# Layer-norm moments, roots and scaling of early row tiles made by the preceding stage at four boundaries of a 17-stage kernel, and the recurrence's projections reordered

## Chip, cores and metric

One core of a Trainium2 chip runs the whole kernel as one program. The metric is the device time of one execution in microseconds (us). Its engines are PE (TensorE, matmuls; PEld is its weight load), DVE (VectorE), ACT (ScalarE), POOL (GpSimd) and SP (SyncE, which here only issues DMAs and clears semaphores).

## What is computed

Two layers over 16 sequences of 64 rows, width 256 (1024 rows in all), with 16 heads of 16 channels. Every one of the six sub-layers starts from a layer norm (without or with gain) of the current `x`:

```python
x = x + cross_attention(ctx, layernorm(x), Wq, Wk, Wv, Wo, bo)      # stage a0
x = x + gated_recurrence(layernorm(x), ...)                          # p2, r1, r2
x = x + ffn(layernorm(x)):  h = x' + self_attention(LN1(x'));        # inputs, a1
                            h + moe(LN2(h))  (8 experts, top 2)      # m1
x = x + plain_cross_attention(layernorm(x), ctx, ctx, w_proj)        # a2
x = x + latent_attention(layernorm(x), W_D*, W_U*, rope)             # p9, a3
x = x + adapters(layernorm(x), W_base, W_enc, W_dec, W_down, W_up)   # p13
```

The recurrence of p2 to r2 needs `k` divided by its per-head length, `a = -k*gamma*f`, and pairs of time steps joined to one.

## The kernel before

Rows lie in SBUF as 8 tiles of 128 rows x 256 channels (`NT` = 8, two sequences to a tile) in one tensor, `X` (for the self-attention `Y`). Each stage is a `Block`: every engine has its own list of instructions, written out by hand in Python order, engines meet only at counting semaphores, and all of them meet at the end of a block. So nothing of a stage starts before the last instruction of the stage ahead.

The class `Normed` (line 105) holds a layer norm. Per tile: `moments` (DVE `bn_stats`, L122), `variances` (DVE `bn_aggr`, L128), for two tiles at a time `roots` (ACT Sqrt, L132) and `inverses` (DVE reciprocal, L136), then `scale` (DVE, (x - mean) * rstd, L142), `turn` (two PE transposes into PSUM, L149) and `take` (ACT copies the turned tile to `xnT`, L156 or L159). `turn(t)` waits for `scaled` of t and for `taken` of t - 2.

The stages that matter here, with the tensor prefix that the profile shows:

- a0, `first_attention_stage` (`a_`): 16 sequences n. For each n: PE scores (L1281), DVE maxima (L1436), ACT exponentials (L1374), PE transposes of the probabilities (L1290), copies out of PSUM by DVE (L1442, three of four) and ACT (L1381), PE values (L1304), POOL `spread_out` (L1209). After an odd n, DVE `heads` (L1452, L1456), then PE `output` (L1317), then in the next, even n DVE `add` to X (L1461). The last tile's `heads` and `add` end the stage. For n up to 12, PE also projects keys and values of sequence n + 3.
- p2, `recurrence_projections_stage` (`p_`, `rec_`): 8 turned tiles; products in the order of `RJOBS` through 4 PSUM banks, two chunks c of 512 columns; ACT takes each product out. DVE makes squares, inverse lengths, fadings, units and decays. POOL makes `decays_twice` (L393), `faded_twice` (L420) and the products with keys (L398, L402). PE `by_heads` (L493, L498) of chunk 0 feeds DVE `next_decays` to `queries` (L329 to L347), which free the banks for `by_heads` of chunk 1; the gate products (L466) come last.
- a1 and a3, `batch_attention_stage`: 4 groups u of 4 sequences (2 tiles). DVE: shifts, sums (L2079), reciprocals, and `add` (L2091) of group u - 2; after the loop `add(2)`, `add(3)`. POOL multiplies by the reciprocals (L2019, 4 x 1 us per group). `output(u)` on PE (L1997) waits for `add(u - 1)`.
- m1, `moe_stage` (`m_`): layer norm of `Y` into `xn`, then, on DVE, `choices` (starting with the copy L2185) and `first_places` per pair of tiles, the token lists, the gathers, and the experts.
- a2, `plain_context_attention_stage`: like a0, without projections; DVE `maxima` (L1791), `heads` (L1807) at even n, `add` (L1816) at odd n. Four of its own tiles are scaled at n = 4 (L1841), after roots by POOL (`inverse_roots`, L1607 and L1610: add eps, power -0.5).
- p9, `latent_inputs_stage`: layer norm, `turn` 0 to 3, products with `D_low` (L2494) and on. POOL starts with a memset of `vblk` (L2609).
- p13, `adapters_stage`: layer norm, `turn` 0 to 3, products with `F_enc` (L2692) and on to the end.

In p2, m1, p9 and p13 the whole layer norm of all eight tiles lies inside the stage, as this loop on DVE:

```python
for g in range(NT // 2 + 1):
    if g < NT // 2: normed.moments(dve, 2 * g); normed.moments(dve, 2 * g + 1)
    if g >= 1: normed.inverses(dve, g - 1)
    if g < NT // 2: normed.variances(dve, g)
    if g >= 1: normed.scale(dve, 2 * g - 2); normed.scale(dve, 2 * g - 1)
```

Of the kernel before, what the change touches and what calls it, by code (L numbers as in the profile page):

```python
# [13 lines left out]
P = 128  # L14
# [147 lines left out]

def norm_project_stage(nc, stage, src, eps, ident, xnT, jobs=(), N=512, gain=None, shift=None, keep=None, clear=None):
# [70 lines left out]
def recurrence_projections_stage(nc, stage, X, eps, ident, xnT, W, rows, r, low, gate, own_cols, both, first_values):  # L234
# [14 lines left out]
    with Scope(nc, stage) as sc:  # L249
        normed = Normed(nc, sc, "x", X, eps, ident, xnT)  # L250
        acc = [sc.ps(f"acc{j}", [P, N]) for j in range(RING)]
        n_ps = [sc.ps(f"n_ps{j}", [P, N]) for j in range(KD)]
        length, inverse = (sc.sb(n, [P, 2, KD, CH, HH]) for n in ("length", "inverse"))
# [26 lines left out]
        with sc.block() as block:  # L280

            @block.vector
            def _(dve):
# [6 lines left out]
                def inverse_lengths(c, m):  # L290
                    dve.wait_ge(n_taken, ONE + KD * c + m + 1)
                    nc.vector.tensor_scalar(length[:, c, m, :, :], length[:, c, m, :, :], 1e-12, None, ALU.max).then_inc(len_ready, 1)
                    dve.wait_ge(len_ready, ONE + KD * c + m + 1)
                    nc.vector.reciprocal(inverse[:, c, m, :, :], length[:, c, m, :, :]).then_inc(inv_ready, 1)
                    dve.wait_ge(inv_ready, ONE + KD * c + m + 1)
                    nc.vector.tensor_copy(wide[:, c, m, :, :, :], inverse[:, c, m, :, :].unsqueeze(3).to_broadcast([P, CH, HH, HD])).then_inc(n_ready, 1)

                def fadings(c, m):

                    wait_read(dve, c, f"g{m}")  # L300
                    nc.vector.tensor_tensor(r["gamma"][:, m, cols(c)], r["gamma"][:, m, cols(c)], r["k"][:, m, cols(c)], ALU.mult).then_inc(part_ready, 1)
                    dve.wait_ge(part_ready, ONE + KD * c + m + 1)
# [46 lines left out]
                for g in range(NT // 2 + 1):  # L349
                    if g < NT // 2:  # L350
                        normed.moments(dve, 2 * g)
                        normed.moments(dve, 2 * g + 1)
                    if g >= 1:
                        normed.inverses(dve, g - 1)
                    if g < NT // 2:
                        normed.variances(dve, g)
                    if g >= 1:
                        normed.scale(dve, 2 * g - 2)
                        normed.scale(dve, 2 * g - 1)
                for c in range(2):  # L360
                    for m in range(KD):
                        squares(c, m)
                for c in range(2):
                    for m in range(KD):
                        inverse_lengths(c, m)
                for c in range(2):
                    for m in range(KD):
                        fadings(c, m)
                    for m in range(KD):
                        units(c, m)  # L370
                        decays(c, m)
# [13 lines left out]
            def _(pool):  # L385
# [3 lines left out]

                def decays_twice(c, m):  # L390
                    pool.wait_ge(k_done, ONE + KD * c + m + 1)
                    wait_read(pool, c, f"f{m}")
                    nc.gpsimd.tensor_tensor(r["k_sig"][:, m, cols(c)], r["f"][:, m, cols(c)], r["f"][:, m, cols(c)], ALU.mult).then_inc(twice_ready, 1)  # L393
# [27 lines left out]

                for c in range(2):
                    for m in range(KD):
                        activated(c, m)
                for c in range(2):
                    for m in range(KD):
                        decays_twice(c, m)
                for c in range(2):
                    faded_twice(c)
# [8 lines left out]
                for c in range(2):  # L438
                    faded_keys(c)

# [2678 lines left out]
```

## Time and profile before

| | |
|---|---|
| median of 3 runs | 897.19 us (897.19 to 898.05) |
| the profiled execution | 897.43 us, of which the span of instructions is 895.6 us |
| PE / DVE / ACT / POOL busy | 763.5 / 570.1 / 429.0 / 316.5 us |
| a0 | 0 to 166.1 us |
| p2 | 166.4 to 235.8 |
| a1, then m1 | to 479.8, 480.1 to 629 |
| a2, then p9 | 630 to 747.1, 747.4 to 782.7 |
| a3, then p13 | 783 to 825.1, 825.4 to 895.6 |

How to read it: times count from the start of the span. A timeline row gives start, duration, engine, line and operation, the tensors as out<-in, how many instructions it merges, and in square brackets how long the engine had been idle and who ended that. An fp32 matmul shows as two records. "PEclk" is the granted TensorE clock: 1.00 is 2.4 GHz, 0.50 is 1.2 GHz.

### The profile page before, as it was taken

The numbers are of one execution on the slowest core, as the hardware profiler recorded it, in microseconds if no ns is written. First come the engines' busy times: TensorE is split into PE (matmuls) and PEld (weight loads), VectorE is DVE, ScalarE is ACT, GpSimd is POOL, SyncE is SP. The second block draws the span as 40 slices with busy tenths as digits, with TensorE's granted clock in tenths as the row PEclk, the third lists the DMA queues.
The fourth block names the chain that finished last, engine by engine and source line by source line (L and its number), as shares of the span: only waits on it lengthen the run. The fifth ranks groups of instructions, "written<-read, shape, count | busy, mean of one in ns | idle before, by whom it ended". The sixth has DMA issues, their size and how long they took to land. (4 is left out here: it accounts for less than half of the span.)

```text
span 895.6 us, 19146 instructions
## 1 busy us (share of the span) xinstructions
PE 763.5 (85%) x7000; PEld 510.2 (57%) x7000; DVE 570.1 (64%) x1295; ACT 429.0 (48%) x1281; POOL 316.5 (35%) x380
## 2 busy tenths in 40 slices
PE   6999999697999999967777299999388896777996
PEld 5788887444433333345456288888267773365334
DVE  3565556539699999976795533232697775465484
ACT  3756666462574665235365100000368882755572
POOL 2211121027477887731351350100564431233002
PEclk9999999798699999989898599999689997979899
DMA  8111700000020000000001036552465310000001
GB/s 260 38 41 53 271 14 1 2 1 1 23 72 0 1 1 1 0 1 0 2 2 48 25 129 179 182 156 72 145 200 195 100 37 1 1 3 3 0 1 49
DMA packets 44893, 51.79 MB, mean 58 GB/s; under 512 B 7072, under 2 KB 40832, under 8 KB 44544
## 3 DMA queue, kind: packets, MB, share of 16 engines
q1 hardware_dynamic: 40256, 43.48, 15.4%
q0 software_dynamic: 1536, 4.20, 1.6%
q10 hardware_dynamic: 3008, 2.88, 0.9%
q8 instruction: 57, 0.93, 0.4%
q14 instruction: 36, 0.29, 0.1%
HBM read 45.31 MB, written 5.24 MB: 56 GB/s over the span
## 5 line engine op out<-in xcount | busy, mean ns | idle before, releaser
L968 PE MATMUL r_u_ps<-r_t_in,l_same_head 128*128 128x512 f32 x124 | 69.4, 641 | 1.0
L936 POOL TENSOR_TENSOR r_q_in<-r_state,rec_q 128x512 f32<-128x512 f32 x62 | 68.1, 1098 | 0.0
L1374 ACT ACTIVATE a_prob<-a_s_ps,a_negmax 128x256 f32<-128x256 f32 x128 | 59.2, 488 | 17.7 <-DVE a_negmax L1436 17.7
L1755 ACT ACTIVATE a_prob<-a_s_ps,a_negmax 128x256 f32<-128x256 f32 x128 | 58.7, 485 | 18.3 <-DVE a_negmax L1791 18.3
L2352 PE MATMUL m_h_ps<-m_rowsT,l_w 128*128 128x256 f32 x256 | 58.7, 390 | 0.0
L1442 DVE COPY a_probT<-a_w_ps 128x512 f32<-128x512 f32 x48 | 31.4, 687 | 39.0 <-PE a_w_ps L1290 39.0
L2352 PEld LDWEIGHTS m_h_ps<-m_rowsT,l_w 128*128 128x128 f32 x256 | 50.2, 197 | 7.3
L2363 PE MATMUL m_y_ps<-l_w,m_hidden 128*128 128x256 f32 x240 | 53.9, 379 | 0.0
L2398 ACT ACTIVATE m_rowsT<-m_xt_ps,l_B_s,l_B_g 128x256 f32<-128x256 f32 x16 | 8.2, 561 | 93.1 <-PE m_xt_ps L2340 93.1
L2266 DVE TENSOR_SCALAR m_hidden<-m_h_ps,l_b 128x256 f32<-128x256 f32 x64 | 28.0, 479 | 37.8 <-PE m_h_ps L2352 37.8
L1791 DVE TENSOR_REDUCE a_negmax<-a_s_ps 128x2 f32<-128x512 f32 x64 | 40.9, 681 | 17.1 <-PE a_s_ps L1671 17.1
L926 POOL TENSOR_TENSOR r_faded<-r_state,rec_both 128x256 f32<-128x256 f32 x62 | 39.9, 643 | 33.2 <-DVE r_state L905 33.2
L1436 DVE TENSOR_REDUCE a_negmax<-a_s_ps 128x2 f32<-128x512 f32 x64 | 39.7, 683 | 16.2 <-PE a_s_ps L1281 16.2
L2363 PEld LDWEIGHTS m_y_ps<-l_w,m_hidden 128*128 128x128 f32 x240 | 45.1, 190 | 5.9
L1209 POOL TENSOR_TENSOR a_spread<-a_rden,all_half 128x256 f32<-128x256 f32 x16 | 9.9, 616 | 105.0 <-DVE a_rden L1448 105.0
L896 DVE TENSOR_TENSOR r_update<-r_u_ps,rec_k 128x512 f32<-128x512 f32 x64 | 44.4, 693 | 1.5 <-PE r_u_ps L962 1.5
L892 DVE TENSOR_TENSOR r_t_in<-r_state,r_par_ps 128x512 f32<-128x512 f32 x62 | 42.6, 687 | 3.2
L2019 POOL TENSOR_TENSOR a_prob<-a_prob,a_rden 128x512 f32<-128x512 f32 x32 | 32.4, 1044 | 34.4 <-DVE a_rden L2085 34.4
L2290 POOL DMA_INDIRECT m_rows<-routed_rows,m_token x16 | 15.4, 966 | 79.7 <-PE m_xt_ps L2340 43.5
L1680 PE MATMUL a_w_ps<-all_ident,a_prob 128*128 128x128 f32 x256 | 38.5, 296 | 3.4 <-ACT a_prob L1755 2.4
L1239 PE MATMUL a_w_ps<-a_ctxT,l_A_WkT 128*128 128x256 f32 x128 | 33.3, 405 | 7.8 <-DMA l_A_WkT<-in_A_WkT 5.9
L968 PEld LDWEIGHTS r_u_ps<-r_t_in,l_same_head 128*128 128x128 f32 x124 | 18.9, 189 | 33.1 <-DVE r_t_in L892 29.6
(388 smaller groups left out, 1899.9 us busy)
## 6 DMA issues: line engine op xcount, KB each, us to landing
l_w<-in_B_w SPq DMA_DIRECT2D x16, 1024.0 KB, 5.9
a_ctxT<-in_ctxT SPq DMA_DIRECT2D x31, 256.0 KB, 2.9
a_ctx<-in_ctx SPq DMA_DIRECT2D x16, 256.0 KB, 2.7
expert_out<-m_y ACTq DMA_DIRECT2D x7, 256.0 KB, 5.8
all_X<-in_x SPq DMA_DIRECT2D x4, 256.0 KB, 5.4
l_b<-in_B_b SPq DMA_DIRECT2D x1, 1024.0 KB, 6.6
all_xnT<-own_rows SPq DMA_DIRECT2D x1, 1024.0 KB, 5.5
routed_rows<-ffn_xn SPq DMA_DIRECT2D x8, 128.0 KB, 1.8
```

Of the source, the lines that this page charges most:

```text
L892: nc.vector.tensor_tensor(t_in[m][:, :, :, :], twice(state[n % 2][m]), a, ALU.mult).then_inc(t_ready[m], 1)
L896: nc.vector.tensor_tensor(update[m][:, :, :, :], u_ps[m][:, :, :, :], steps("k", 2 * n, 2, m), ALU.mult).then_inc(upd_ready[m], 1)
L926: nc.gpsimd.tensor_tensor(faded[m][:, :, :], state[n % 2][m][:, :, :], f, ALU.mult).then_inc(faded_ready[m], 1)
L936: ins = nc.gpsimd.tensor_tensor(q_in[i % 2][m][:, :, :, :], twice(state[i % 2][m]), steps("q", 2 * i - 1, 2, m), ALU.mult)
L968: nc.tensor.matmul(u_ps[m][:, :, :, :], same_head[:, :], t_in[m][:, :, :, :], start=False, stop=True).then_inc(u_mm[m], 1)
L1374: ins = nc.scalar.activation(prob[n % 2][:, r, m, :], s_ps[r][:, m, :], ACT.Exp, bias=negmax[n % 2][:, r, m:m + 1], accum_out=den[n % 2][: ...
L1436: nc.vector.tensor_reduce(negmax[n % 2][:, r, :], s_ps[r][:, :, :], AX.X, ALU.max, negate=True).then_inc(max_ready, 1)
L1680: mm = nc.tensor.transpose(acc[:, (2 * m + c) * P:(2 * m + c + 1) * P], prob[n % 2][:, r, m, c * P:(c + 1) * P], ident[:, :])
L1755: ins = nc.scalar.activation(prob[n % 2][:, r, m, :], s_ps[r][:, m, :], ACT.Exp, bias=negmax[n % 2][:, r, m:m + 1], accum_out=den[n % 2][: ...
L1791: nc.vector.tensor_reduce(negmax[n % 2][:, r, :], s_ps[r][:, :, :], AX.X, ALU.max, negate=True).then_inc(max_ready, 1)
L2352: mm = nc.tensor.matmul(h_ps[i][:, f, :], w1[j][:, k, (2 * i + f) * P:(2 * i + f + 1) * P], rowsT[j][:, k, :], start=(k == 0), stop=(k == ...
L2363: mm = nc.tensor.matmul(y_bank(e, slice(c, c + 1))[:, 0, :], hidden[j][:, f, c * P:(c + 1) * P], w2[j][:, f, :], start=(f == 0), stop=(f = ...
```

## The change

1. A subclass `EarlyNormed` is created before the stage ahead. It has `find_moments` (DVE `bn_stats`, a wait, `bn_aggr`), `root` (POOL: add eps, a wait on itself, power -0.5; no ACT and no DVE reciprocal) and `scale_row` (as `scale`, waiting for the root). `begin` gives it the PSUM banks when the stage that uses it starts; `turn` and `take` stay there.
2. a0 finds moments, roots and scales tiles 0 to 5 for p2 inside its loop (odd n from 3: moments of n//2 - 1 before `heads`, root on POOL after `spread_out`; even n from 4: scaling of n//2 - 2 after `maxima`), with the root of tile 6. p2 is left with moments and root of tile 7 and the scaling of 6 and 7.
3. a1 (for m1) and a3 (for p13): after the loop, tiles 0 to 3 between `add(1)` and `add(2)`, moments and root of 4 and 5 between `add(2)` and `add(3)`. m1 and p13 are left with scaling 4 and 5 and everything of 6 and 7.
4. a2 does tiles 0 to 6 for p9: at even n from 4 the moments after `heads`, at odd n from 5 the scaling after `add`. p9 is left with tile 7, whose root on POOL stands ahead of the memset.
5. ACT in p2, m1, p9, p13 loses its roots, and so the load of the Sqrt table there (p2 keeps the Sqrt for `lengths`).
6. In p2: `decays_twice` moves from POOL to ACT (Square, after each `f`); `lengths` are two activations for both chunks, `inverse_lengths` are two 64-wide bounds, two reciprocals and four copies; all `fadings` of both chunks come ahead of all `units`; `faded_twice(1)` moves to the end of POOL's list; PE does `v0` and `v1` of chunk 0 before `spread(1)`, and `by_heads(0)` after `v0` of chunk 1.
7. r1's `raw` and `own_rows` lie in the space of the scaled rows.

```diff
+class EarlyNormed(Normed):
+    def find_moments(self, dve, t):
+        self.moments(dve, t)
+        dve.wait_ge(self.moments_ready, ONE + t + 1)
+        self.nc.vector.bn_aggr(self.meanvar[:, t, :], self.parts[:, t, :]).then_inc(self.var_ready, 1)
+    def root(self, pool, lo, hi):
+        pool.wait_ge(self.var_ready, ONE + hi)
+        self.nc.gpsimd.tensor_tensor(self.std[:, lo:hi], self.meanvar[:, lo:hi, 1], self.eps[:, 0:1].to_broadcast([P, hi - lo]), ALU.add).then_inc(self.widened, 1)
+        self.raised += 1
+        pool.wait_ge(self.widened, ONE + self.raised)
+        pool.wait_ge(self.exponent_ready, ONE + 1)
+        self.nc.gpsimd.tensor_tensor(self.rstd[:, lo:hi], self.std[:, lo:hi], self.minus_half[:, 0:1].to_broadcast([P, hi - lo]), ALU.pow).then_inc(self.rstd_ready, hi - lo)
+    def scale_row(self, dve, t):
+        dve.wait_ge(self.rstd_ready, ONE + t + 1)
...
# p2, DVE (the loop over g is gone)
+                normed.find_moments(dve, NT - 1)
+                normed.scale_row(dve, NT - 2)
+                normed.scale_row(dve, NT - 1)
...
                 for c in range(2):
                     for m in range(KD):
                         fadings(c, m)
+                    for m in range(KD):
+                        faded_gammas(c, m)
+                for c in range(2):
                     for m in range(KD):
                         units(c, m)
                         decays(c, m)
# p2, PE
-                product(0, "v0")
+                for name in ("v0", "v1"):
+                    product(0, name)
                 for m in range(KD):
                     spread(1, m)
-                product(0, "v1")
+                product(1, "v0")
                 by_heads(0)
-                for name in ("v0", "v1"):
-                    product(1, name)
+                product(1, "v1")
                 by_heads(1)
# p2, ACT
+                    if name in ("f0", "f1"):
+                        decays_twice(c, int(name[1]))
# a0, POOL and DVE
                     spread_out(n)
+                    if n % 2 == 1 and n >= 3:
+                        following.root(pool, n // 2 - 1, n // 2)
...
+                    if n % 2 == 1 and n >= 3:
+                        dve.wait_ge(x_added, ONE + n // 2)
+                        following.find_moments(dve, n // 2 - 1)
                     if n % 2 == 1:
                         heads(n // 2)
+                    if n % 2 == 0 and n >= 4:
+                        following.scale_row(dve, n // 2 - 2)
# a2, DVE
+                    if n % 2 == 0 and n >= 4:
+                        dve.wait_ge(x_added, ONE + n // 2 - 1)
+                        following.find_moments(dve, n // 2 - 2)
+                    if n % 2 == 1 and n >= 5:
+                        following.scale_row(dve, n // 2 - 2)
# a1 and a3, DVE
+                dve.wait_ge(x_added, ONE + NU - 2)
+                for t in range(NT - 4):
+                    following.find_moments(dve, t)
+                for t in range(NT - 4):
+                    following.scale_row(dve, t)
                 add(NU - 2)
+                dve.wait_ge(x_added, ONE + NU - 1)
+                for t in (NT - 4, NT - 3):
+                    following.find_moments(dve, t)
                 add(NU - 1)
# m1, DVE (p13 the same)
+                for t in (NT - 4, NT - 3):
+                    normed.scale_row(dve, t)
+                for t in (NT - 2, NT - 1):
+                    normed.find_moments(dve, t)
+                for t in (NT - 2, NT - 1):
+                    normed.scale_row(dve, t)
# p9, POOL
+                normed.root(pool, NT - 1, NT)
                 nc.gpsimd.memset(vblk[:, :, :, :], 0.0).then_inc(zeroed, 1)
```

## Rows read from the trace of the kernel before

**Rows 1.** The page: busy time, share of the span, instructions of each engine.
```profile
PE 763.5 (85%) x7000; PEld 510.2 (57%) x7000; DVE 570.1 (64%) x1295; ACT 429.0 (48%) x1281; POOL 316.5 (35%) x380
```
**Rows 2.** Timeline across a0 to p2: last add, first turns, first product.
```profile
165.68 0.42 DVE L1461 TENSOR_TENSOR all_X<-a_w_ps,all_X 128x256 f32<-128x256 f32 x1 [1.22 <-PE a_w_ps L1317]
...
168.69 1.12 PE L149 MATMUL p_x_turned<-all_ident,p_x_rows 128*128 128x128 f32 x4 [3.05 <-DVE p_x_rows L142]
...
170.55 0.72 PEld L149 LDWEIGHTS p_x_turned<-all_ident,p_x_rows 128*128 128x128 f32 x4 [1.15 <-DVE p_x_rows L142]
...
172.26 3.78 PE L454 MATMUL p_acc<-all_xnT,l_R_Wk 128*128 128x512 f32 x4 [0.59 <-ACT all_xnT L156]
```
**Rows 3.** Timeline at a1 to m1: the last adds, layer norm, first choices.
```profile
475.16 0.69 DVE L2091 TENSOR_TENSOR ffn_Y<-a_out_ps,ffn_Y 128x512 f32<-128x512 f32 x1 [4.58 <-PE a_out_ps L1997]
...
477.11 1.99 PE L1997 MATMUL a_out_ps<-l_B_Wo,a_headsT 128*128 128x256 f32 x8 [0.96 <-ACT a_headsT L2043]
...
480.16 0.75 DVE L122 BATCH_NORM_STATS2 m_x_parts<-ffn_Y 128x6 f32<-128x256 f32 x2 [0.32 <-PEq L1944]
...
486.44 0.17 DVE L2185 COPY m_logits<-m_h_ps 128x16 f32<-128x16 f32 x1
```
**Rows 4.** Timeline of p9's start: memset, first turns, first product.
```profile
747.37 3.51 POOL L2609 MEMSET mla_vals<- 128x4096 f32 x1 [5.47 <-POOLq L1565]
...
748.30 0.72 DVE L122 BATCH_NORM_STATS2 p_x_parts<-all_X 128x6 f32<-128x256 f32 x2
...
749.23 2.12 DVE L142 TENSOR_SCALAR p_x_rows<-all_X,p_x_meanvar,p_x_rstd 128x256 f32<-128x256 f32 x2
...
751.09 1.12 PE L149 MATMUL p_x_turned<-all_ident,p_x_rows 128*128 128x128 f32 x4 [4.45 <-DVE p_x_rows L142]
...
756.03 3.78 PE L2494 MATMUL p_banks<-all_xnT,l_D_low 128*128 128x512 f32 x4 [0.47 <-ACT all_xnT L156]
```
**Rows 5.** Timeline at a3 to p13: first turns and the first two products.
```profile
827.72 0.76 PE L149 MATMUL p_recon<-all_ident,p_x_rows 128*128 128x128 f32 x4 [3.30 <-DVE p_x_rows L142]
...
831.29 3.78 PE L2692 MATMUL p_acc<-all_xnT,l_F_enc 128*128 128x512 f32 x4 [0.96 <-ACT all_xnT L156]
...
835.29 1.96 PE L2692 MATMUL p_acc<-all_xnT,l_F_enc 128*128 128x512 f32 x4
```
**Rows 6.** Windows: busy PE, PEld, DVE, ACT, POOL; then PEclk, DMA share, GB/s.
```profile
163.00:166.40 3.40, 1.67 (x8) 1.07 (x8) 1.27 (x3) 0.01 (x1) 0.00 (x0) 1.00 0.00 0
...
746.80:750.10 3.30, 0.00 (x0) 0.00 (x0) 2.98 (x11) 1.88 (x3) 2.73 (x1) 1.00 0.01 2
...
815.20:818.80 3.60, 2.48 (x17) 1.77 (x18) 0.91 (x4) 1.80 (x3) 3.04 (x4) 1.00 0.00 0
```
**Rows 7.** POOL's power of four numbers per partition (groups by line and form).
```profile
L1610 POOL TENSOR_TENSOR a_x_rstd<-a_x_std,a_minus_half 128x4 f32<-128x4 f32 x1 | 1.1, 1054 | 0.1
```
**Rows 8.** DVE in a0's tail (heads of n = 13) and a2 (n = 4, 5, 8).
```profile
151.79 0.41 DVE L1452 COPY a_factor<-a_o_ps 128x256 f32<-128x256 f32 x1
...
682.37 1.29 DVE L1791 TENSOR_REDUCE a_negmax<-a_s_ps 128x2 f32<-128x512 f32 x2
...
688.34 1.29 DVE L1791 TENSOR_REDUCE a_negmax<-a_s_ps 128x2 f32<-128x512 f32 x2 [1.90 <-PE a_s_ps L1671]
...
705.85 1.29 DVE L1791 TENSOR_REDUCE a_negmax<-a_s_ps 128x2 f32<-128x512 f32 x2 [1.23 <-PE a_s_ps L1671]
```
**Rows 9.** Groups of p2's middle (198 to 218 us), costliest first.
```profile
L304 DVE TENSOR_TENSOR rec_gamma<-rec_gamma,rec_k_sig 128x512 f32<-128x512 f32 x4 | 5.4, 1346 | 0.1
...
L301 DVE TENSOR_TENSOR rec_gamma<-rec_gamma,rec_k 128x512 f32<-128x512 f32 x4 | 5.0, 1256 | 0.0
...
L308 DVE TENSOR_TENSOR rec_k<-rec_k,p_n_ps 128x512 f32<-128x512 f32 x4 | 2.7, 677 | 0.0
```
**Rows 10.** Timeline of p2's end: chunk 0 joined, `by_heads(1)`.
```profile
218.31 0.70 DVE L329 TENSOR_TENSOR p_n_ps<-p_x_turned,rec_a 128x512 f32<-128x512 f32 x1
...
223.15 2.05 PE L493 MATMUL p_x_turned<-p_q_with_k,l_same_head 128*128 128x512 f32 x2 [4.87 <-DVE rec_q L347]
```

More of the change, by code:

```diff
@@ L160, in take, with __init__, begin, prepare @@
         ins.then_inc(self.taken, 1)
+class EarlyNormed(Normed):
+    def __init__(self, nc, sc, name, src, eps, keep, ring=NT):
+        super().__init__(nc, sc, name, src, eps, keep=keep)
+        self.ring = ring
+        self.minus_half = sc.sb(f"{name}_minus_half", [P, 1])
+        self.exponent_ready, self.widened = (sc.sem(f"{name}_{n}") for n in ("exponent_ready", "widened"))
+        self.raised = 0
+    def begin(self, sc, name, ident, xnT, gain=None, shift=None, turned_ps=None):
+        self.ident, self.xnT, self.gain, self.shift = ident, xnT, gain, shift
+        self.turned_ps = turned_ps if turned_ps is not None else [sc.ps(f"{name}_turned{j}", [P, 2 * KD, P]) for j in range(2)]
+        self.turned, self.taken = sc.sem(f"{name}_turned"), sc.sem(f"{name}_taken")
+    def prepare(self, pool):
+        self.nc.gpsimd.memset(self.minus_half[:, :], -0.5).then_inc(self.exponent_ready, 1)
+    def find_moments(self, dve, t):
[11 more added lines that the diff above has]
+        dve.wait_ge(self.rstd_ready, ONE + t + 1)
+        if t >= self.ring:
+            dve.wait_ge(self.turned, ONE + t - self.ring + 1)
+        self.nc.vector.tensor_scalar(self.rows[:, t % self.ring, :], self.src[:, t, :], self.meanvar[:, t, 0:1], self.rstd[:, t:t + 1], ALU.subtract, ALU.mult).then_inc(self.scaled, 1)
 def norm_project_stage(nc, stage, src, eps, ident, xnT, jobs=(), N=512, gain=None, shift=None, keep=None, clear=None):
@@ L368, in _ @@
                         fadings(c, m)
+                    for m in range(KD):
+                        faded_gammas(c, m)
+                for c in range(2):
                     for m in range(KD):
@@ L424, in _ @@
                         activated(c, m)
[L425 to L429, printed above, removed]
+                faded_twice(0)
                 queries_with_keys(0)
@@ L439, in _ @@
                     faded_keys(c)
+                faded_twice(1)
             @block.tensor
@@ L2552, in place_keys @@
                     nc.scalar.activation(k_rope[:, c * HB:(c + 1) * HB, e, :], plain_k[c][:, :, :], ACT.Copy, scale=quad[:, e:e + 1]).then_inc(kr_ready, 1)
-                for g in range(NT // 2):
-                    normed.roots(act, g)
                 for t in range(4):
```

181 lines of the change are left out of this document (79 added, 102 removed).

## Prediction, made before the changed kernel was run

> **What bounds the kernel now.** PE is busy for 85% of the span [rows 1], but that is a mean over 17 stages; I read the table of windows first, to find the stretches where PE is not full, and then the timeline across each of the four changed boundaries. All of them look alike. The last add of the stage ahead ends, and PE has nothing until DVE has gone through moments, the roots on ACT, the reciprocals and the scaling of two tiles, and then waits again between pairs. Between a0 and p2 the add ends at 166.1, PE's first turn starts at 168.69, the second pair at 170.55, the first product at 172.26 [rows 2]. Between a2 and p9 the same takes from 747.4 to 756.03, since two scalings take 2.12 us while the memset on POOL runs, where other DVE passes over 128x256 take 0.4 each [rows 4, 8]. p13 starts at 825.4 and its first product at 831.29 [rows 5]. In m1 DVE itself is the bound: `choices` starts at 486.44, when the last scaling is issued, 6.3 us after DVE began with the moments at 480.16 [rows 3]. What comes behind each of these points is a PE or DVE list that runs nearly without holes, so a start that is earlier by so much should end the stage earlier by as much. The sum is therefore made of four starts, of what the stages ahead pay for the added work, and of the middle of p2.
>
> **Start of p2.** With tiles 0 to 5 scaled in a0, the first turn can start at about 166.4. From the second pair's start to the product, 170.55 to 172.26, are 1.71 us [rows 2]; `turn(2)` waits for `taken(0)`, which is a turn at 1.2 GHz (0.56 us, half of the 1.12 for two) [rows 2], some 0.1 to be seen, and one copy by ACT (estimated at 0.4 to 0.45, as DVE's copy of 128x256 takes 0.41 [rows 8]): `turn(2)` at 167.6, product at 169.3. Gain 172.3 - 169.3 = 3.0. ACT has no roots and no table load ahead of its copies any more. What is left on DVE (one `find_moments`, two scalings, one root between them) is some 2.5 us and ends at 169, and these tiles are turned only beside products.
>
> **Price in a0.** Five of the six moments and all scalings stand in slack: PE is the bound while it projects keys and values, and `find_moments` is short: `bn_stats` about 0.4 (two of them 0.72 [rows 4]) and a `bn_aggr` of a few numbers, estimated at 0.2 from the 16-number copy of 0.17 [rows 3]; 0.6 together. In the tail it is not: at n = 13 the heads start at 151.79 right behind the maxima [rows 8], the output product, two transposes and the scores of the last sequence follow from them through the ring of three banks. I charge the whole 0.6. At n = 15 DVE waits for PE in any case; at n = 14 a scaling of 0.4 is caught up within the copies. POOL's `root` waits for DVE with `queries` and `add_bias` queued behind it, and PE waits for those; they are wanted about a sequence later. Together +0.6.
>
> **Middle of p2.** POOL's squares, products with keys and the two `faded_twice` run beside DVE's `fadings`. Those 8 multiplications took 1346 and 1256 ns on average, those with one operand in PSUM 677 ns [rows 9]: 10.4 against 5.4 us. The Trainium skill (SBUF — State Buffer, "SBUF: two separate sides") says that a VectorE instruction with two SBUF inputs and a GpSimd one exclude each other for their whole length; the trace agrees here, where no multiplication of two SBUF operands ran at its short time beside POOL's. After the change only `faded_twice(0)`, some 1.3 us, meets them. Placing the steps one by one in old time: `fadings` of both chunks end near 207.5 instead of 215.7, but `units(0)` are later by 0.5, `spread(1)` waits for `v0` and `v1` (two products of 1.9) and ends at 213.3, `units(1)` and `decays(1)` end at 215.2 instead of 218.1. Now PE is late: `v0` of chunk 1 and `by_heads(0)` take 1.9 + 2.0, so `next_decays` starts at 217.3 instead of 218.31 [rows 10]. The rest of the 2.9 us goes there. DVE's seven operations and `by_heads(1)` follow as before: -1.0. ACT's four added squares of 0.6 hold the last take of `f` by about 1 us, behind which nothing waits longer than DVE does. At the bounds: nothing at all if ACT's squares hold the products (their bank waits), -4 if PE's clock holds (below).
>
> **Start of m1, price in a1.** DVE had idled for 4.58 us ahead of `add(2)` at 475.16 [rows 3]. Into it go four moments (2.3 us, 470.6 to 472.9; POOL is still multiplying, but `bn_stats` beside a memset took 0.72 for two as ever [rows 4]), one root of four, an addition estimated at 0.2 and the power of 1.05 [rows 7], to 474.4 with the hops between them, and four scalings, to 475.9. `add(2)` is 0.7 late and ends at 476.6, ahead of the product at 477.11 that needs it (that one waits for ACT) [rows 3]. So the cover is 0.5 us wide, and what overruns it costs one for one. In m1 remain two scalings (0.7), two moments (1.2), a root of two (about 1.2 with hops) and two scalings (0.7): from 480.2 to 484.1 instead of 486.44. `choices(0)` starts there, since the logits of two tiles are ready at about 483. Gain 2.3 to 2.5; I take 2.4. The list behind it is DVE-bound up to the token lists.
>
> **Start of p9, price in a2.** First turn at 747.4, product at 750.2 at 1.2 GHz by the working of p2: 756.0 - 750.2 = 5.8. The memset now comes after a root and may hold the scaling of tile 7, wanted 10 us later. In a2, at even n, the moments (0.6) go into a gap of 1.23, at odd n the scaling (0.4) into one of 1.90 [rows 8]. By the skill's rule above a scaling there, if it counts as an instruction that needs POOL's port, may wait out `spread_out`'s 0.6; then it takes 1.0 of the 1.90 and the sum stays. At n = 4 there is no gap: four own scalings run up to the maxima at 682.37 [rows 8]. There +0.6. In the tail, `find_moments(5)` of n = 14 and the rest fit into waits for PE. Net -5.2.
>
> **Start of p13, price in a3.** As a1, the same instructions 345.5 us later, with a slack of 0.3. First turn at 825.4 instead of 827.72 [rows 5], product at 827.5 (PE is still at 2.4 GHz, turns of 0.3 us) instead of 831.29: -3.8. All behind it runs off PE.
>
> Sum with PE's clock as it was: -3.0 + 0.6 - 1.0 - 2.4 - 5.2 - 3.8 = -14.8.
>
> **The clock.** Each of these gaps costs twice. In the stretch 746.8 to 750.1 PE did nothing at a clock of 1.00 [rows 6], and the first product then took 3.78 us; p13's second product took 1.96 at the full clock against 3.78 of the first [rows 5]. What did PE do where the clock stayed? From 815.2 to 818.8 it was busy 2.48 of 3.60 at 1.00. What where it fell? After 163.0 to 166.4 with 1.67 of 3.40 [rows 6]. In p13 PE will turn four tiles (1.2 us) and be in products from 827.5, before the clock fell: I expect it to hold, -1.9. In p9 turns and then products fill about 1.7 to 2.3 of the former idle 3.3: between the two rows. I take it that it holds, -2.1 (one product 1.9, and a little of the next). At p2's start it fell before the changed part begins; no gain taken. At p2's end PE idles 4.87 us ahead of `by_heads(1)`, which took 2.05 for one product [rows 10], twice its fast time; the idle time shrinks to about 3.2; I expect it to fall still, but if not, `by_heads(1)` and the gates behind it give 3 us more.
>
> -14.8 - 1.9 - 2.1 = -18.8. From the profiled execution's 897.4 that is 878.6; the median of the runs, 897.19, is 0.2 lower than that execution. New semaphores and two POOL operations a tile add a few tenths: 878.7.
>
> **Rivals.** (A) The forecast, 878.7: chance 0.42. (B) The clock holds at neither boundary: 897.4 - 14.8 = 882.6, chance 0.25. For it: 1.67 of 3.40 busy was not enough at 166.4. (C) It holds at p2's end too, or rises sooner at p2's start because turns now follow each other: 875.5, chance 0.15. (D) The change does only half of what it says: the starts are earlier, but the added work stands on the path in a1, a3 and a2's tail, whose slacks are 0.3 to 0.6 us by my reckoning, each of the three overrun by about 1.5, and p2's middle gives nothing, since ACT, not DVE, ends last: -14.8 + 4.5 + 1.0 = -9.3, 888, chance 0.11. (E) Slower: the wait of DVE's `scale_row` and of POOL's `root` for each other ties two in-order lists in a0 and a2. The mechanism is POOL standing in `root` with `spread_out` or the values' copies behind it, until DVE comes past its maxima; it decides once such a round trip exceeds a2's gap of 1.23 us [rows 8]. To outweigh 18.8 us and 1.8 more, each of 13 tiles would have to lose 1.6 us net, so moments, root and scaling (0.6 + 0.8 + 0.4, and hops) would have to stand on the path nearly whole every time: 899 to 901, chance 0.04. (F) No difference within 0.2%: D with half of E's losses, 0.03.
>
> What a run can tell from no change is about 0.2%, 1.8 us. Faster than that are A to D, 0.93; within 0.03; slower 0.04. Predicted time 878.7. The range goes from C's lower side (p2's end at -4) to D: 872.5 to 889.0; it leaves out E, F and the edges of C and D.
>
> **What would show it.** First turns within 0.4 us of each stage's start; first products of p2, p9 and p13 about 3.2, 3.1 and 2.4 us behind the last add instead of 6.2, 8.9 and 6.1; `choices` 4.0 us behind m1's start instead of 6.3; `output(3)` at unchanged distance in a1 and a3; the cycle of a2 still 5.8 us a sequence; PEclk 1.00 in the first 4 us of p9 and p13; L301 and the second multiplication at about 0.7 us each. I am wrong if `add(2)` delays `output(3)`, if a2's cycle grows, or if p2 from first product to end is not shorter by 1 us.

## The result, and the profile after the change

The changed kernel takes 873.63 us (median of 4 runs, 872.39 to 875.87) against 897.60 of the kernel before on the same chip: a ratio of 0.974, 95% interval 0.972 to 0.976. Beside the last experiment it ran again: 877.03 against 901.23, a ratio of 0.973 (0.971 to 0.976). The prediction was 878.7 with a range of 872.5 to 889.0. The direction and the range hold, and the kernel gained 24 us where 18.5 were forecast. Its profiled execution took 873.75, with a span of 872.0.

The page of the changed kernel, its busy line and the clock in 40 slices:

```profile
PE 754.6 (87%) x7000; PEld 503.2 (58%) x7000; DVE 567.9 (65%) x1275; ACT 418.8 (48%) x1261; POOL 329.7 (38%) x424
...
PEclk9999999898699999988989589999879999989999
```

PE has as many matmuls as before [rows 1] and is busy for 8.9 us less: nothing was taken from its list, and its mean granted clock is 0.935 instead of 0.920, so I count that part of the gain as clock. The rest is idle time that is gone. To see where, I marked the same instructions in both traces (last adds, first products, PE's first instruction of r1 and a3) and took the differences. Lengths in us:

| stretch | before | after | difference | forecast |
|---|---|---|---|---|
| start to a0's last add | 166.10 | 165.60 | -0.50 | +0.6 |
| to p2's first product | 6.16 | 2.88 | -3.28 | -3.0 |
| p2 from there to r1 | 63.80 | 60.25 | -3.55 | -1.0 |
| r1, r2, p5, a1 to its last add | 243.78 | 244.02 | +0.24 | 0 |
| m1, to a2's first turn | 159.48 | 156.33 | -3.15 | -2.4 |
| a2 to its last add | 107.77 | 108.13 | +0.36 | +0.6 |
| to p9's first product | 8.94 | 2.46 | -6.48 | -5.8 |
| p9 from there to a3 | 26.96 | 26.52 | -0.44 | -2.1 |
| a3 to its last add | 42.16 | 40.97 | -1.19 | 0 |
| to p13's first product | 6.14 | 2.46 | -3.68 | -3.8 |
| p13 from there to the end | 64.31 | 62.38 | -1.93 | -1.9 |
| sum | 895.6 | 872.0 | -23.6 | -18.8 |

The boundary a0 to p2 in the timeline of the changed kernel answers to [rows 2] (start, duration, engine, line, operation; in brackets the idle time before it and who ended it):

```profile
165.18 0.42 DVE L1504 TENSOR_TENSOR all_X<-a_w_ps,all_X 128x256 f32<-128x256 f32 x1 [1.22 <-PE a_w_ps L1360]
165.94 0.67 PE L149 MATMUL p_x_turned<-all_ident,n_rows 128*128 128x128 f32 x4 [0.80 <-PEq L1204]
166.92 1.09 PE L149 MATMUL p_x_turned<-all_ident,n_rows 128*128 128x128 f32 x4 [0.31 <-DVE n_rows L199]
...
168.48 3.78 PE L491 MATMUL p_acc<-all_xnT,l_R_Wk 128*128 128x512 f32 x4 [0.47 <-ACT all_xnT L156]
```

The first turn waits only for the stage's start (0.34 us behind the add), and ACT, not DVE, is named ahead of the product. The 0.31 us ahead of the second pair of turns are put down to DVE, but the scaling of 0.40 us that ended at 166.90 is tile 6's, which that turn does not need. The first product runs at 1.2 GHz (3.78 us for its four matmuls) as before. m1's start answers to [rows 3], on DVE:

```profile
473.08 0.74 DVE L199 TENSOR_SCALAR ffn_xn<-ffn_Y,ffn_x_meanvar,ffn_x_rstd 128x256 f32<-128x256 f32 x2 [0.32 <-PEq L2004]
...
476.03 0.74 DVE L199 TENSOR_SCALAR ffn_xn<-ffn_Y,ffn_x_meanvar,ffn_x_rstd 128x256 f32<-128x256 f32 x2 [1.14 <-POOL ffn_x_rstd L193]
476.68 0.17 DVE L2257 COPY m_logits<-m_h_ps 128x16 f32<-128x16 f32 x1
...
478.09 0.17 DVE L2257 COPY m_logits<-m_h_ps 128x16 f32<-128x16 f32 x1
```

p9's start answers to [rows 4]: the gap is gone, but the product takes 3.65 us, so PE ran at 1.2 GHz, and tile 7's scaling lasts as long as the memset beside it.

```profile
738.51 0.68 PE L149 MATMUL p_x_turned<-all_ident,l_rows 128*128 128x128 f32 x4 [0.35 <-ACT all_xnT L156]
...
739.02 3.51 POOL L2664 MEMSET mla_vals<- 128x4096 f32 x1
739.11 3.57 DVE L199 TENSOR_SCALAR l_rows<-all_X,l_latent_meanvar,l_latent_rstd 128x256 f32<-128x256 f32 x1 [0.93 <-POOL l_latent_rstd L193]
739.67 3.65 PE L2559 MATMUL p_banks<-all_xnT,l_D_low 128*128 128x512 f32 x4 [0.47 <-ACT all_xnT L156]
```

The windows behind the last adds of a2 and a3 (busy PE, PEld, DVE, ACT, POOL; then PEclk, DMA share, GB/s) answer to [rows 6]:

```profile
737.20:739.70 2.50, 1.34 (x9) 0.85 (x9) 1.21 (x4) 1.32 (x4) 1.37 (x3) 1.00 0.01 3
739.70:743.30 3.60, 3.60 (x5) 1.54 (x6) 2.98 (x1) 0.00 (x0) 2.83 (x1) 0.53 0.00 0
...
807.20:809.60 2.40, 1.31 (x8) 0.82 (x8) 1.75 (x6) 1.32 (x4) 0.19 (x1) 1.00 0.00 0
809.60:813.60 4.00, 3.98 (x13) 1.98 (x14) 1.83 (x8) 0.99 (x3) 0.69 (x1) 1.00 0.00 0
```

PE was as busy behind a2 as behind a3 (1.34 of 2.50 and 1.31 of 2.40), and yet the clock fell in p9 and stayed at 1.00 in p13. p2's end answers to [rows 10]:

```profile
212.99 0.70 DVE L374 TENSOR_TENSOR p_n_ps<-p_x_turned,rec_a 128x512 f32<-128x512 f32 x1 [1.85 <-PE p_x_turned L535]
...
217.82 2.05 PE L530 MATMUL p_x_turned<-p_q_with_k,l_same_head 128*128 128x512 f32 x2 [3.15 <-DVE rec_q L392]
...
221.29 4.16 PE L503 MATMUL p_acc<-l_R_up,rec_low 16*128 16x256 f32 x16
```

`next_decays` now waits for PE, as forecast, and PE's wait ahead of `by_heads(1)` is 3.15 instead of 4.87.

### The profile page after: what moved, and what is told of

Its sections match the earlier page's. It is cut to its first block and busy times, and to the rows that moved or that the text cites. A ratio compares the mean times of both kernels' runs of the same rounds, so it can differ in the third digit from the quotient of the medians.

```text
span 872.0 us, 19156 instructions
## 1 busy us (share of the span) xinstructions
PE 754.6 (87%) x7000; PEld 503.2 (58%) x7000; DVE 567.9 (65%) x1275; ACT 418.8 (48%) x1261; POOL 329.7 (38%) x424
## 3 DMA queue, kind: packets, MB, share of 16 engines
q10 hardware_dynamic: 3008, 2.88, 1.0%
## 5 line engine op out<-in xcount | busy, mean ns | idle before, releaser
L1807 ACT ACTIVATE a_prob<-a_s_ps,a_negmax 128x256 f32<-128x256 f32 x128 | 58.6, 483 | 18.8 <-DVE a_negmax L1843 18.8
L2333 DVE TENSOR_SCALAR m_hidden<-m_h_ps,l_b 128x256 f32<-128x256 f32 x64 | 28.0, 480 | 37.8 <-PE m_h_ps L2420 37.8
```

Source lines behind the costliest of these rows:

```text
L1807: ins = nc.scalar.activation(prob[n % 2][:, r, m, :], s_ps[r][:, m, :], ACT.Exp, bias=negmax[n % 2][:, r, m:m + 1], accum_out=den[n % 2][: ...
```

## The experiments

Profiles of one kernel differ by more than the terms in dispute: in a2's first sequences by up to 6 us (a2 takes 108.13 and 112.34 in two executions of the changed kernel; the cause was not followed up), and in p5 and p2 by 1 to 2 us with the clock. So the totals alone do not settle a term of 3 us, and I compare the stretches of the table. Each ratio is against the kernel before in the same session.

**The four boundaries, one at a time.** Each kernel is the changed one with one boundary undone:

```
-  first_attention_stage(..., early)          # undo_p2: an object that does nothing
+  first_attention_stage(..., NotYet())
   # p2: normed.find_moments / scale_row / root(pool)  ->  moments, variances, roots(act), inverses, scale
```

and the same for a1/m1, a2/p9 and a3/p13.

> The changed kernel with the first boundary alone undone: a0 does nothing for p2, p2 finds all moments, roots on ACT and scalings itself as before; the new order of its body stays. By the additive theory a0's last add comes 0.5 to 0.6 earlier against n = 13's maxima (no moments ahead of the heads), the first product stands 6.2 us behind the last add again instead of 2.9, and p2 from first product to its end stays at 60.3: 873.6 + 3.3 - 0.55 = 876.3. Rival: the parts hang together through PE's clock, and the body changes its length with the start, by 2 to 3 us either way: 873.5 to 874.5 or 878.5 to 879.5.

> The changed kernel with the boundary a1 to m1 alone undone. Additive theory: choices start 6.5 us behind m1's start instead of 3.6 to 3.9, the second ones another 0.4 later, output(3) of a1 stays where it is: 873.6 + 3.1 = 876.7. Rival (the early moments overran their cover in a1 and cost there about 1.5): a1 becomes shorter by 1.5 and the whole is 875.2. What m1 has behind the choices should keep its length in both.

> The changed kernel with the boundary a2 to p9 alone undone. Additive theory: first product 8.9 us behind the last add instead of 2.5, it takes 3.8 us (clock low, as it is with the change too, 3.65), a2 shorter by 0.4: 873.6 + 6.9 - 0.4 = 880.1. a3 was 1.2 us shorter in the changed kernel, because the clock rose by its second scores (0.96 instead of 0.50 in that stretch); if that hangs on where p9 starts, it goes too and the time is 881.3; if it is of another origin, a3 stays at 41.0 us.

> The changed kernel with the boundary a3 to p13 alone undone. Additive theory: first product 6.1 us behind the last add instead of 2.5 and it takes 3.8 us at the low clock instead of 2.0 at the full one: 873.6 + 3.7 + 1.9 = 879.2. Rival: the clock's part is not the boundary's doing, and the first product is fast again though the gap is back: 877.3.

| undone | median, ratio | what came back in its own stretch |
|---|---|---|
| p2 | 883.76, 0.980 (0.975 to 0.984) | first product 6.16 behind the last add; heads of n = 11 to n = 13 of a0 16.26 instead of 16.88 |
| m1 | 881.35, 0.978 (0.975 to 0.982) | `choices` 6.61 behind the last add instead of 3.93; all of m1 158.95 instead of 155.7 to 155.9 |
| p9 | 884.07, 0.982 (0.977 to 0.987) | first product 8.93 instead of 2.46; the rest of p9 26.59, no longer than with the change (26.51 to 27.13) |
| p13 | 884.05, 0.981 (0.978 to 0.984) | first product 6.14 instead of 2.46 and at 3.78 us instead of 1.98; the rest 65.02 instead of 62.1 to 63.0 |

The kernel before took 900.38 beside them. Against the 0.974 of the changed kernel the ratios lie 4.1 to 7.4 us higher, with intervals of some 3 to 5 us each way. Those of p9 and p13 lie clear of the changed kernel's interval (0.972 to 0.976), those of p2 and m1 just touch it, so by the totals alone the gain of these two is likely and no more. All four totals also came out 0.9 to 2.6 us longer than expected. In the profiled executions some of it lies where nothing was undone: a2 takes 111.86 to 114.16 instead of 108.13 with p2, m1 or p13 undone, and with p2 undone r1 to a1 takes 247.48 instead of 244.02. The stretches say how much each boundary is worth, and they are those of the additive theory: 3.0 (6.16 less the 3.12 of the other three) less 0.6, then 3.1, 6.5, and 3.7 with 2 to 3 of clock. The product of p13 with its boundary undone:

```profile
816.41 1.05 PE L149 MATMUL p_recon<-all_ident,l_rows 128*128 128x128 f32 x4 [0.74 <-DVE l_rows L142]
818.48 3.78 PE L2762 MATMUL p_acc<-all_xnT,l_F_enc 128*128 128x512 f32 x4 [1.02 <-ACT all_xnT L156]
```

Its four matmuls take 3.78, so the clock is low, as in the kernel before; in the twelve profiled executions with early tiles there it was at the full clock every time, 1.98 to 1.99 for all four. The rival that the clock is not that boundary's doing has fallen. In p9 it is the other way: with and without the change the rest of p9 is equally long here. a3 stayed at 40.7 to 41.2 in three of the four, the one with a3's own early work undone among them (41.04), and took 42.08 in one that did not touch it. So no single boundary accounts for its 1.2 us, and where they come from stays open.

**p2's order.** The changed kernel with p2's body in the order of before; then the changed kernel with only the squares of `f` back on POOL:

```
-                    if name in ("f0", "f1"): decays_twice(c, int(name[1]))      # ACT, Square
+                nc.gpsimd.tensor_tensor(k_sig, f, f, ALU.mult)                # POOL, four times, ahead of faded_twice(0)
```

> The changed kernel with p2's body (order of PE's products, DVE's steps and POOL's squares) as it was before; the early tiles stay. If the new order is what shortened p2's body, it takes 63.8 us from first product to end again instead of 60.2: 873.6 + 3.6 = 877.2. If a part of it came from the earlier start (another phase of PE's clock), the body stays below 62.5: under 876. At by_heads(1) PE should then have idled some 4.9 us again instead of 3.15, and the gates behind it should run at half the clock.

> The changed kernel, in which only the four squares of f go back from ACT to POOL; all other orders are the new ones. Theory 1, the gain of the middle came from DVE and POOL no longer meeting over SBUF operands: L344 and L349 take 1.2 to 1.4 us each again instead of 0.7, units(0) come 2.5 to 3 later, and the body is 62.3 to 63.2. Theory 2, it came from PE's new order (v0 and v1 ahead of spread(1), v0 of chunk 1 ahead of by_heads(0)) and the merged lengths: DVE has 2.7 us of idle time ahead of units(1), which hide what is lost, and the body stays within 0.6 of 60.2.

old_order: 875.84, ratio 0.977 (0.975 to 0.979). squares_on_pool: 874.51, ratio 0.976 (0.974 to 0.978). The body took 62.23 and 58.36. Neither number can be read before the clock is set apart. In p2 it falls while PE makes the products of `g` and `f`, which have 16 rows of operand, and again at the stage's end. By the granted clock in the traces the first of these low stretches lasts from 28.3 to 35.1 us behind the first product in the kernel before and from 28.6 to 35.5 in the changed one, but from 27.6 to 37.8 in old_order and from 23.6 to 33.8 in squares_on_pool, whose first product was at the full clock. So I compare steps that lie within one engine's hands. From `by_heads(0)` on PE to `next_decays` on DVE: 5.34 us before, 3.76 with the old order in the changed kernel, 1.92 in all twelve kernels with the new order, squares_on_pool too. In squares_on_pool DVE's multiplications met POOL again:

```profile
L344 DVE TENSOR_TENSOR rec_gamma<-rec_gamma,rec_k 128x512 f32<-128x512 f32 x4 | 5.1, 1312 | 0.0
L349 DVE TENSOR_TENSOR rec_gamma<-rec_gamma,rec_k_sig 128x512 f32<-128x512 f32 x4 | 4.2, 1100 | 0.0
```

against 687 and 880 ns in the changed kernel (groups of lines, mean ns of one), 3.1 us more of busy time in all. But `units(1)` waited 2.69 us for PE in the changed kernel and 0.62 here, and that hid it: from the first `spread` to `by_heads(0)` squares_on_pool took 10.69, the changed kernel 10.35. Theory 2 holds: the gain of the middle is not that of the squares on ACT, and the meeting of DVE and POOL, which I had put first, costs 0.3 in this pair. It comes from what is left of the new order: PE's products, the merged `lengths`, and all `fadings` ahead of `units`. No run takes these three apart. In the totals the intervals of both kernels overlap with the changed kernel's.

With the clock in the same pattern the new order is worth this: `by_heads(1)` starts 50.89 us behind the first product before and 49.34 after (clock low from 28.3 to 35.1 and from 28.6 to 35.5), but 50.39 with the old order and 50.15 with the new one in heads_first (low from 27.6 to 37.8 and from 27.5 to 37.7). It gains 1.6 in the one pattern and 0.2 in the other, where the low stretch is the longer one. Each of these is one execution.

**The gates ahead of by_heads(1).**

```
                product(1, "v1")
+               for name in ("gate0", "gate1"):
+                   product(0, name)
                by_heads(1)
-               for c in range(2): gates of c
+               for name in ("gate0", "gate1"):
+                   product(1, name)
```

> The changed kernel, in which PE makes the two gate products of chunk 0 ahead of by_heads(1) instead of behind it, so that its idle 3.15 us there hold 2 us of work. Theory 1, the clock falls because of that gap: by_heads(1) then runs at the full clock (1.0 instead of 2.05), A's product ends 1.6 to 1.9 earlier, ACT has two takes less behind it, and r1 starts 1.7 to 2.5 earlier: 873.6 - 2.1 = 871.5. Theory 2, the clock falls regardless of what fills the gap: by_heads(1) takes 2.05 still, only the gates' own 1 to 2 us are gained on PE, and since ACT and DVE end the stage, r1 is earlier by at most 0.6: 873.0.

873.61, ratio 0.975 (0.973 to 0.976): in the total no gain over the changed kernel. The stretch to compare is heads_first's, whose clock had the same pattern: `by_heads(1)` at 50.15 and 50.07, r1 at 61.85 and 59.13.

```profile
215.81 1.99 PE L503 MATMUL p_acc<-l_R_up,rec_low 16*128 16x256 f32 x8
219.03 1.10 PE L530 MATMUL p_x_turned<-p_q_with_k,l_same_head 128*128 128x512 f32 x2 [1.24 <-DVE rec_q L392]
219.97 1.68 PE L535 MATMUL p_x_turned<-p_a_with_k,l_same_head 128*128 128x512 f32 x2
221.57 3.78 PE L503 MATMUL p_acc<-l_R_up,rec_low 16*128 16x256 f32 x8
```

PE's wait is down to 1.24 from 3.15, and the clock falls all the same in the second product of `by_heads(1)` (1.68 here and 1.60 in heads_first, instead of 1.02). So theory 1 has fallen: that gap is not what lowers it. The windows of the changed kernel show how little PE's busy share says here. The clock fell at 224.4 though PE had been busy with the gate products for all of the 3.00 us ahead of it:

```profile
221.40:224.40 3.00, 3.00 (x14) 2.59 (x15) 2.93 (x5) 1.68 (x4) 0.50 (x1) 1.00 0.00 0
224.40:228.40 4.00, 1.05 (x3) 0.31 (x1) 2.58 (x7) 4.00 (x13) 0.00 (x0) 0.50 0.00 0
```

The 2.7 us come by way of ACT, which neither theory had: in heads_first its twelve copies of the first values start at 225.74, behind a take of a slow gate product that ends at 225.85, and r1 begins when ACT has done the last takes; here they start at once.

```profile
223.14 3.73 ACT L597 ACTIVATE all_QT<-rec_v,l_diag 128x128 f32<-128x128 f32 x12 [4.71 <-DVE rec_v L368]
226.67 1.10 ACT L579 ACTIVATE rec_gate<-p_acc 128x512 f32<-128x512 f32 x2
```

**The price in a0.** At odd n the heads ahead of the early moments:

```
-                    if n % 2 == 1 and n >= 3: x_added wait; following.find_moments(...)
                     if n % 2 == 1: heads(n // 2)
+                    if n % 2 == 1 and n >= 3: x_added wait; following.find_moments(...)
```

> The changed kernel, in which DVE computes in a0 the heads ahead of the early moments instead of behind them (at every odd n). From the heads of n = 11 to those of n = 13 are 16.88 us in the changed kernel and 16.33 before; if the moments ahead of the heads are the price, it is 16.3 again and the last add comes 0.55 to 0.6 earlier: 873.6 - 0.6 = 873.0, with at most 0.2 of it given back at n = 15. Rival: the moments then delay the transposed copies of the next sequence by as much, and nothing is gained. The last output took 1.13 us in one execution and 2.07 in three others, depending on whether the clock had fallen ahead of it; 0.6 earlier should make the first the rule, which is worth another 0.95.

874.50, ratio 0.974 (0.972 to 0.977). DVE in a0's tail:

```profile
151.66 0.41 DVE L1495 COPY a_factor<-a_o_ps 128x256 f32<-128x256 f32 x1
152.10 0.42 DVE L1499 TENSOR_TENSOR a_headsT<-a_o_ps,a_factor 128x256 f32<-128x256 f32 x1
152.44 0.42 DVE L122 BATCH_NORM_STATS2 n_x_parts<-all_X 128x6 f32<-128x256 f32 x1
...
163.83 0.42 DVE L1495 COPY a_factor<-a_o_ps 128x256 f32<-128x256 f32 x1 [2.58 <-PE a_o_ps L1353]
```

From the heads of n = 11 to those of n = 13 are 16.34 instead of 16.88: the price was where the prediction had it. But the next pair, to n = 15, takes 12.17 instead of 11.76, since the moments now stand ahead of the transposed copies. Net 0.13: mostly the rival.

**The covers.** More of the added work: four `bn_stats` (unused) behind the four early scalings of a1 and a3, and the power three times in each root of one tile.

```
+                for i in range(4):
+                    nc.vector.bn_stats(spare[:, i, :], X[:, 0, :])
...
+        if hi - lo == 1:
+            for i in range(2): self.nc.gpsimd.tensor_tensor(self.spare[...], self.std[:, lo:hi], minus_half, ALU.pow)
```

> The changed kernel with more of the added work, to measure its covers. (1) In a1 and a3 DVE makes four more bn_stats (some 1.5 us, results unused) behind the four early scalings. In the changed kernel add(2) ends 0.8 us ahead of output(3) in a1 and 0.6 ahead in a3, which both waited for ACT. By the forecast's theory the cover is that wide and no wider: output(3) comes 0.7 to 0.8 later in a1 and 0.9 to 1.0 in a3, and the waits then name DVE. If PE doesn't wait for add(2) there at all, neither moves. (2) Each root of one tile makes the power three times (1.1 us more on POOL, 13 times in a0, p2, a2 and p9). By the forecast's theory POOL's list has room: the cycles of a0 and a2 stay at 5.76. By rival E, DVE's scaling and POOL's root tie the lists, and each pair of sequences grows by up to 1 us, a2 by 5 to 6 in all. Sum by the forecast's theory 873.6 + 1.7 = 875.3, by E 886.

875.80, ratio 0.976 (0.972 to 0.980). PE's last outputs of a1 and a3:

```profile
471.28 1.53 PE L2064 MATMUL a_out_ps<-l_B_Wo,a_headsT 128*128 128x256 f32 x6 [1.60 <-DVE ffn_Y L2162]
...
806.10 1.75 PE L2064 MATMUL a_out_ps<-l_D_WO,a_headsT 128*128 128x256 f32 x7 [1.59 <-DVE all_X L2162]
```

From `output(2)` to `output(3)` a1 takes 4.53 instead of 3.88 and a3 4.51 instead of 3.64, and the wait names DVE's add. The covers are some 0.8 and 0.6 us wide, and what overruns them costs one for one. a2's cycle stays at 5.75 to 5.77 us with 1.1 us more on POOL in each root: rival E has no footing at three times the power's price.

**Work for PE at the boundaries.** Transposes of the identity, read by nobody, in PE's waits:

```
+   in a0 and a2:  warm(work_bank(("out", t)), 4)  ahead of the last output; in a0 2 ahead of each transposition of n = 15
+   in p2 and p9:  warm(bank, 1) ahead of turn(0), warm(bank, 2) behind turn(1), warm(bank, 3) behind turn(3)
```

> The changed kernel with transposes of the identity, whose results nobody reads, put into PE's waits at two boundaries: in a0's tail two ahead of each transposition of the last sequence and four ahead of the last output, in a2's tail four ahead of the last output, and at the head of p2 and of p9 one ahead of the first turn, two behind turn(1) and three behind turn(3). Theory 1, the clock falls there because of what PE left undone: p9's first product takes 1.9 instead of the 3.6 it took in seven looks with early tiles, and p2's too (3.5 to 3.8 in eight of nine), the clock reads 1.00 through both boundaries: 873.6 - 1.7 - 1.7 = 870.2. Theory 2, so few transposes do not change it: both first products as they were, 873.6. Theory 3, they come into the way of what they precede: the last outputs later by 0.3 and more, 874.5.

872.71, ratio 0.971 (0.969 to 0.974). PE at p9's start:

```profile
738.41 0.38 PE L2600 MATMUL p_banks<-all_ident 128*128 128x128 f32 x2
738.92 0.68 PE L149 MATMUL p_x_turned<-all_ident,l_rows 128*128 128x128 f32 x4
739.44 0.49 PE L2600 MATMUL p_banks<-all_ident 128*128 128x128 f32 x3
740.08 1.98 PE L2581 MATMUL p_banks<-all_xnT,l_D_low 128*128 128x512 f32 x4
```

```profile
737.50:740.10 2.60, 1.99 (x15) 1.50 (x15) 1.31 (x4) 1.32 (x4) 1.47 (x3) 1.00 0.01 3
740.10:744.10 4.00, 4.00 (x10) 1.85 (x11) 3.16 (x2) 0.60 (x1) 2.73 (x1) 1.00 0.02 4
```

Theory 1 holds for both first products: they take 1.98 to 1.99, and p9 from there to a3 24.82 instead of 26.52. In the total the intervals of this kernel and the changed one overlap. Then both gains together, beside the changed kernel itself.

> The two edits that gained locally, together: the identity's transposes at both boundaries and the gates of chunk 0 ahead of by_heads(1). If they add up, p2 takes 57.5 us from first product to r1 (the transposes alone 60.15, the gates alone 59.13 after a start at the low clock), p9 24.8, and the whole is 872.7 - 2.6 = 870.1, ratio to before 0.969. If the clock only moves its low stretches to other places, p2 stays at 59 and more and the ratio at 0.971 or above.

> The changed kernel itself once more, beside the version above: 873.6, ratio to before 0.9736. p9's first product at the low clock (3.6 us), p13's at the full one (2.0), first product of p2 2.5 to 3.1 us behind the last add; p2 60 to 62 us and the last output of a0 either 1.1 or 2.1 us, by where the clock's steps fall.

gates_and_warm: 875.63 against 901.23, ratio 0.971 (0.969 to 0.973). The changed kernel beside it: 877.03, ratio 0.973 (0.971 to 0.976). p2 takes 57.06 and p9 24.86, so both gains add up locally: r1 begins 3.5 us sooner. The whole gains 1.4. Of the 3.5, r2 and p5 take 1.3 back in the profiled execution (54.19 us against 52.86; p5 alone 28.64 instead of 26.64), a3 takes another 0.8 (42.02 against 41.18), and p9 gave nothing there, since this execution of the changed kernel had the full clock at p9 without any help:

```profile
744.45 1.98 PE L2559 MATMUL p_banks<-all_xnT,l_D_low 128*128 128x512 f32 x4 [0.47 <-ACT all_xnT L156]
```

Over all profiled executions with early tiles at that boundary: without the transposes the product was fast in 1 of 10 at p9 and in 1 of 10 at p2, with them in 2 of 2 at each. The intervals of the two versions overlap; that it beats the changed kernel is likely, not shown.

## Why the prediction came out as it did

**The starts (right).** First turns stand 0.34, 0.32, 0.33 and 0.32 us behind the last adds; first products of p2, p9 and p13 2.88, 2.46 and 2.46 instead of the forecast 3.2, 3.1 and 2.4. p9's working took the clock as fallen by the second pair of turns, while the clock's term counted on it to hold: the two do not go together. It fell only when the product began, so the turns were fast: -6.5 instead of -5.8, and that is paid back in the product.

**m1 (right in kind, 0.7 short).** `choices` 3.6 us behind m1's start instead of 4.0, since the root of two costs 0.19 + 0.69 and its hops are short. The second `choices` follows 1.4 us later instead of 1.9: PE had turned the first tiles before DVE was done. The stretch came out at -3.15; undoing it gave 3.1.

**The prices (right in place and size).** a0 paid 0.55 to 0.6 at n = 13 and a2 0.36. Five of the seven scalings in a2 took 0.64 beside `spread_out` instead of 0.4, less than the 1.0 that the working allowed, and the cycle took it. The -0.50 of the table is a0's price less 1.0 at the kernel's very start, which is not the change's doing nor the clock's (it rose at 9.4 us in both traces). There, a0's own scalings of tiles 2 and 3 meet POOL's memsets (the first pair of rows from the trace before, the second from that after):

```profile
8.63 2.73 POOL L1213 MEMSET a_vals<- 128x1024 f32 x3 [8.18 <-issue]
9.57 2.25 DVE L142 TENSOR_SCALAR a_x_rows<-all_X,a_x_meanvar,a_x_rstd 128x256 f32<-128x256 f32 x2
...
8.68 3.02 POOL L1254 MEMSET a_vals<- 128x1024 f32 x3
9.38 1.43 DVE L142 TENSOR_SCALAR a_x_rows<-all_X,a_x_meanvar,a_x_rstd 128x256 f32<-128x256 f32 x2
```

In three of the fourteen profiled executions (the changed kernel's first, squares_on_pool and warm) the first of the two scalings took 0.4 and both were done at 10.8 us; in the other eleven they were done at 11.7 to 11.8, and all that follows in a0 is 0.9 to 1.0 later. a1's and a3's covers were 0.8 and 0.6 wide where I had 0.5 and 0.3, and `output(3)` had 0.96 and 0.72 of idle time before it, as before. The cycle of a2 stayed at 5.8.

**p2's middle (the step that failed).** The forecast was -1.0, the measured -3.55, near the bound of -4. The way was right: PE ends last, and `next_decays` is earlier. Two terms were mis-sized. `next_decays` came 1.5 earlier instead of 1.0. And "I expect it to fall still, but if not, 3 us more" was put as all or nothing. What the trace shows is a third case: the clock falls before `by_heads(1)` (2.05 us, as before), but is up again when the gates begin, whose 16 matmuls take 4.16 instead of 7.19; behind them r1 starts 2.0 sooner. That was in rival C with 0.15. It is not certain to come: the clock was up between `by_heads(1)` and the last gates in nine of the twelve executions of the new order and in neither of the two of the old one, and no run shows that the order is the cause. I had also given the contention of DVE and POOL the first place in the explanation. For the single instruction the trace agrees with the rule of the Trainium skill quoted there (SBUF — State Buffer, "SBUF: two separate sides"): 1312 ns beside POOL, 687 alone, and 880 on average for the second multiplication, since one of the four met `faded_twice(0)` and took 1.46 us. That none ran at its short time beside POOL in the kernel before was read too strictly: two of the eight, which had begun first (at 203.11 and 205.16 us), took 0.68. But the runs show that it was not what the stage waited for.

**The clock (half right).** p13: -1.93 against -1.9, and shown by undoing it. p9: -0.4 against -2.1. The step that failed is the comparison of busy shares: I placed p9 between a row with 1.67 of 3.40, where the clock fell, and one with 2.48 of 3.60, where it held, and took the upper side for both boundaries. At the same busy share p13 held and p9 did not, so the share does not decide it, and what does, these rows do not show. In both executions with the transposes (0.65 us more of work in that stretch, 0.6 in a2's tail) it held.

**What was missed.** -1.2 in a3 and +0.24 in r1 to a1, for which no term of the sum stood. They moved in other kernels as well (a3 from 40.7 to 42.1). Of the 4.8 us between forecast and result 2.6 are p2, 1.2 are a3, 1.1 are a0; the rest nearly cancels. That the rest cancels is luck: the 1.7 us that p9's clock did not give were made up by p9's start and m1, 0.7 each, and p2's start. The 2.2 us of a0's start and a3 have nothing to do with the reasoning; without them the time would be some 876, in the range as well and nearer to the forecast.

## What to carry to other kernels

Layer norm ahead of a projection is a chain of hops between DVE, ACT and PE, and any tile whose rows are complete before the last one can have it done in the stage that completes it: the first product then stands 2.5 to 2.9 us behind the last add instead of 6 to 9. The work fits where DVE waits for PE for longer than it takes, and in a tail it costs one for one. Where a shortened gap leaves the clock at full speed in some executions only, count it as a chance and not as a gain, or give PE matmuls whose results nobody reads there (at p9 and p2 it held in 2 of 2 with them and in 1 of 10 without). And compare stretches at the same clock pattern before crediting an order.

## What I had not expected of the hardware

A scaling of 128x256, which reads one SBUF tensor and writes another, lasted 3.57 us beside a memset of 3.51 (0.41 otherwise): it waited out the whole instruction, not a share. The Trainium skill (SBUF — State Buffer, "SBUF: two separate sides") says that the ports which DVE and POOL share are an exclusive lock for the whole instruction, for a DVE instruction with two SBUF inputs or in a mode that uses both ports. The trace agrees with the lock; which mode the scaling ran in it does not show. At the kernel's start it could go either way: the scaling that began at 9.38 to 9.40 us took 0.4 in three executions and 1.27 in a fourth, where it waited for the next memset. A `bn_stats` beside POOL's multiplications and memsets took its 0.37 to 0.43. POOL's power took 0.55 to 0.58 us for one number a partition, 0.69 to 0.73 for two and 1.02 to 1.05 for four.

The clock was at full speed in one execution and at half in another at the same instruction of the same program: p9's first product took 3.65 and 1.98 us. a0's last output took 1.13 us in both executions of the changed kernel and 2.07 to 2.08 in three kernels that differ from it in later stages only. That alone moves a stage by 1 to 2 us. What decides it I leave open.
